# An attention kernel's output store parted over two DMA queues

## The reference

```python
def _L0_xattn_ref(enc_outputs, dec_outputs):
    a_t = jnp.einsum('bed,btd->bet', enc_outputs, dec_outputs)
    a_t = jax.nn.softmax(a_t, axis=-1)
    return jnp.einsum('bet,bed->btd', a_t, enc_outputs)

def _L0_ffn_ref(x, W, b, V_r, C):
    base = jnp.einsum('bsd,od->bso', x, W) + b
    correction = jnp.einsum('bsr,or->bso', jnp.einsum('bsd,dr->bsr', x, V_r), C)
    return base + correction

x = x + _L0_xattn_ref(ctx_1024, _layernorm(x, axis=-1))       # x 1x128x256, ctx 1x12544x256
x = x + _L0_attn_ref(_layernorm(x, axis=-1), w_attn, b_attn, w_proj, b_proj)   # causal, 16 heads
x = x + _L0_ffn_ref(_layernorm(x, axis=-1), W, b, V_r, C)
return x
```

## Time and profile before

| | us |
|---|---|
| time before, median of 3 executions | 106.11 |
| lowest and highest of them | 105.77, 106.12 |
| the profiled execution, its own time | 105.76 |
| its span, first to last instruction | 103.7 |
| around the span (105.76 - 103.7) | 2.06 |
| TensorE busy | 98.3 (95%) |
| the end of `x3`'s instruction in the profile (101.06 + 0.48) | 101.54 |
| the store, from issue to landing | 1.7 |

### The profile page before, as it was taken

One profiled execution on the slowest core, in us unless ns is written; L12 is line 12 of the kernel. 1 busy time (PEld: TensorE's weight loads), 2 busy tenths in 40 slices (PEclk: granted clock), 3 DMA queues, 4 the chain that ended last, 5 costly groups with the idle time before them and its releaser, 6 DMA issues.

```text
span 103.7 us, 2257 instructions
## 1 busy us (share of the span) xinstructions
PE 98.3 (95%) x740; PEld 86.4 (83%) x740; DVE 76.3 (74%) x217; ACT 72.7 (70%) x268; POOL 63.8 (62%) x46
## 2 busy tenths in 40 slices
PE   5999999999999999999999999999999999969990
PEld 1389999999999999999999999999998976845660
DVE  0412959959999999988777797777889745699641
ACT  4019599599999999997777977778879304489410
POOL 6405499869999999999766797666886001004020
PEclk9999999999999999999999999999999999999999
DMA  3899999999999999999999999993000000000001
GB/s 70 330 417 412 411 411 406 408 408 408 414 400 409 403 416 406 408 409 409 408 406 406 411 408 409 388 369 125 0 0 6 0 0 0 0 0 0 6 0 51
DMA packets 8746, 27.86 MB, mean 269 GB/s; under 512 B 1120, under 2 KB 1824, under 8 KB 8736
## 3 DMA queue, kind: packets, MB, share of 16 engines
q1 hardware_dynamic: 8736, 27.73, 68.3%
HBM read 27.59 MB, written 0.13 MB: 267 GB/s over the span
## 4 chain that ended last, share of the span: by engine, by line
PE 89%; DVE 4%; DMA 2%; issue 1%; POOL 1%; ACT 0%; DVEq 0%
PE bank L323 43%; PE bank L335 21%; PE bank L338 10%; DVE head_max L716 2%; DMA x<-x_dram 2%; PE bank L406 2%; PE bank L443 1%; PE bank L344 1%; PE bank L419 1%; PE bank L500 1%; PE bank L308 1%; PE bank L486 1%; PE bank L389 1%; PE bank L386 1%; PE bank L462 1%
## 5 line engine op out<-in xcount | busy, mean ns | idle before, releaser
L288 POOL TENSOR_TENSOR rows_split<-rows_ring,rows_split 128x1024 fp32r<-128x1024 f32 (+1 forms) x25 | 58.4, 2335 | 16.9 <-ACT rows_split L518 16.8
L323 PE MATMUL bank<-query_t,cols_ring 128*128 128x128 f32 x392 | 47.5, 276 | 0.0
L323 PEld LDWEIGHTS bank<-query_t,cols_ring 128*128 128x128 f32 x392 | 45.7, 192 | 1.3 <-ACT query_t L509 0.3
L529 ACT ACTIVATE bank<-bank,neg_max 128x128 f32<-128x128 f32 x98 | 33.1, 338 | 7.4 <-DVE neg_max L653 7.2
L335 PE MATMUL bank<-rows_split,probs 128*128 128x512 f32 x92 | 34.7, 413 | 0.0
L518 ACT CAST rows_split<-rows_ring 128x1024 fp32r<-128x1024 f32 (+1 forms) x25 | 25.8, 1033 | 6.1 <-DMA rows_ring<-ctx_rows_dram 5.1
L670 DVE SCALAR_TENSOR_TENSOR probs<-bank,inv_sums,probs 128x128 fp32r<-128x128 f32 x98 | 27.6, 345 | 0.9
L338 PE MATMUL bank<-rows_split,probs 128*128 128x256 f32 x92 | 25.6, 279 | 0.0
L653 DVE TENSOR_REDUCE neg_max<-bank 128x4 f32<-128x512 f32 (+1 forms) x25 | 16.8, 672 | 8.6 <-PE bank L323 8.6
L335 PEld LDWEIGHTS bank<-rows_split,probs 128*128 128x128 f32 x92 | 17.3, 189 | 3.1
L529 ACT ACTIVATION_READ_ACCUMULATOR bank<-bank,neg_max 128x1 f32 x98 | 19.8, 202 | 0.0
(11 more groups left out here) (96 smaller groups left out, 64.0 us busy)
## 6 DMA issues: line engine op xcount, KB each, us to landing
cols_ring<-ctx_cols_dram SPq DMA_DIRECT2D x24, 512.0 KB, 14.8
rows_ring<-ctx_rows_dram SPq DMA_DIRECT2D x24, 512.0 KB, 15.2
wqk_sb<-w_qk_dram SPq DMA_DIRECT2D x1, 512.0 KB, 11.6
cols_ring<-ctx_cols_dram SPq DMA_DIRECT2D x1, 256.0 KB, 11.3
rows_ring<-ctx_rows_dram SPq DMA_DIRECT2D x1, 256.0 KB, 12.1
wv_sb<-w_v_dram SPq DMA_DIRECT2D x1, 256.0 KB, 11.7
wproj_sb<-w_proj_dram SPq DMA_DIRECT2D x1, 256.0 KB, 10.4
wffn_sb<-w_ffn_dram SPq DMA_DIRECT2D x1, 256.0 KB, 9.7
```

Source lines behind the costliest of these rows:

```text
L288: pool.tensor_tensor(rows_split[:, b, 0:n, 1, :], rows_ring[:, slot * STEP:slot * STEP + n, :], rows_split[:, b, 0:n, 0, :].bitcast(F32), ...
L323: last = pe.matmul(into[:, t * P:(t + 1) * P], cols_ring[:, slot * STEP + t, c, :], query_t[:, c, :], start=(c == 0), stop=(c == DC - 1))
L529: last = act.activation(on[:, t * P:(t + 1) * P], on[:, t * P:(t + 1) * P], ACT.Exp, bias=neg_max[:, b, t:t + 1], accum_out=sums[:, b, t:t ...
```

## The change

The store is parted by rows. SyncE stores rows 0 to 63 (64 KB), ScalarE rows 64 to 127 (64 KB), each after its own wait for `x3_ready`. Both raise the same semaphore by 16, and SyncE now waits for 32. ScalarE's two instructions stand behind all else in its block. `x3` itself is still written by one instruction of all 128 partitions.

```diff
             sp.wait_ge(x3_ready, 1)
-            sp.dma_start(out, x3[:]).then_inc(out_stored, 16)
-            sp.wait_ge(out_stored, 16)
+            sp.dma_start(out[0:P // 2], x3[0:P // 2]).then_inc(out_stored, 16)
+            sp.wait_ge(out_stored, 32)
...
             for c in range(DC):
                 act.wait_ge(x2_t_ready, c + 1)
                 act.copy(x2_centred_t[:, c, :], x2_t_ps[c][:, 0:P]).then_inc(x2_t_copied, 1)
+
+            act.wait_ge(x3_ready, 1)
+            act.dma_start(out[P // 2:P], x3[P // 2:P]).then_inc(out_stored, 16)
```

## The result

The changed kernel takes 106.49 us (median of 22, 105.92 to 107.52), the kernel before 106.03 (median of 22, 105.46 to 106.46). The ratio is 1.0047 with a 95% interval of 1.003 to 1.0063: it is slower by about 0.5 us, and that is clear of the noise. (The longest reading, 107.52, counts as a slow run, and the ratio leaves it out.) I had forecast no change, +0.1. The time lies in the range, and the difference just inside my half per cent, but the forecast of a change too small to see was wrong.

What follows compares the result with a forecast made beforehand. TensorE, busy 95% of the span, was taken to bound the kernel, with the uncovered store at the end the only part touched. Terms 0 + 0 + 0 + 0.1 + 0 + 0 gave +0.1, forecast 106.1 us, range 105.6 to 106.8.

Steps and rivals of the forecast that it cites:

- What bounds the end: From x3's end to the closing barrier: nothing covers the steps, so any change there goes to the time one for one.
- SyncE's store of 64 rows: SyncE's issue of the half store: same 0.37 us as the whole store's; ends -0.18 and 0, taken as 0.
- The bytes: Moving the store's 131 KB: DMA engines already busy throughout, so the same 0.48 us by either queue; taken as 0.
- When ScalarE's half starts: Start of ScalarE's issue relative to SyncE's: 0 if side by side, +0.17 if in line; taken as +0.1 us.
- ScalarE's wait and issue: ScalarE's new instructions at the end: they delay nobody and its later drain stays hidden before the barrier; no cost.
- the completion: SyncE's wait for 32 counts from two transfers: ends 0 and +0.35 us, taken as 0.
- a queue used for the first time: ScalarE's queue carrying its only transfer: being first costs about 0.1 us, within the +0.1 already taken.
- outside the span: The 2.06 us around the profiled span: a second queue could add 0 to +2.06; taken as 0.
- A: Both issues at once, costing by the row, halves earlier by 0.18: -0.1 to -0.2 us, 105.8 to 106.0; chance 0.27.
- B: ScalarE's issue is dear, handled more slowly than SyncE's: an issue of 1.29 would give +0.68 us, 106.7; chance 0.10.
- C: The second queue lengthens the 2.06 us outside the span: +0.53 to +1, 106.6 to 107.0; chance 0.04.
- D: Waits before and behind the bytes go by a transfer's rows, so half would go: -0.6 us, 105.4; chance 0.04.

## Why the prediction was wrong

*What bounds the end* was right. Nothing covers the string from x3 to the barrier, and the +0.49 in it came out one for one in the time.

*SyncE's store of 64 rows* was the step that failed, and ScalarE's with it, which is of 64 rows too. I bounded it by -0.18 and 0 and took 0, arguing that an issue does not follow the bytes. It does not, yet its shape matters: 0.52 in place of 0.37, and the first bytes, which I tied to the end of the issue, came 0.3 later. My bound from above was no bound. I had excluded a loss because a smaller transfer could surely not cost more, without a row that had its number of partitions. The 0.85 and 1.29 of the 32-row loads I rightly left aside: 32 rows alone took 0.33.

*The bytes* failed as well, and by its own premise. A full share does not mean a full rate. I read the 0.94 to 1.01 in the earlier trace rows as "no gaps, so the same 0.48". The share stayed near 1 (0.77 to 1.10 in the full windows) while the rate fell from 340 to 244 GB/s, about +0.2.

*When ScalarE's half starts* carried my only cost, +0.1, for issues in line. The issues run side by side (0.36 and 0.39 in the store by columns). What goes nearly in line is the bytes: ScalarE's began at least 0.24 behind SyncE's. I had reckoned 0.41 and an idle gap of 0.17. The gap did not come, the second half cost no more than its own bytes, and so this term is about 0. The lock that the Trainium skill's page Trace Analysis, section "DMA Instruction — HWDGE (DVE, Sync)", describes is not to be seen in the length of any issue; whether it is what holds ScalarE's bytes back, no run shows.

*ScalarE's wait and issue*, *the completion*, *a queue used for the first time* and *outside the span* came out as said: 0 or at most the 0.1 of the tail with ScalarE as the only issuer. The drain was hidden though twice as long as I took it, SyncE came 0.4 behind the last byte with 32 counts as with 16, and 2.08 lie around the span.

*The rivals* of the prediction. A, side by side, had the two issues at once right, and their cost by the row and the sign wrong. B gave its slower result to ScalarE; SyncE's issue was as long. C and D did not occur. The Trainium skill's rule on two disjoint partition halves, "Don't bother" (page DMA: Bandwidth & Descriptors, section "Rules for kernel authors"), is borne out and by more than it says: one half alone costs more than the whole.

In sum: I put 0 for the shape of the transfer and +0.1 for the issues in line; the runs showed about +0.3 and +0.2 for the shape and about 0 for the issues. That 106.49 still lies in the range is luck. The likeliest case had ended at 106.4, and what opened the range to 106.8 were rivals B and C, which did not occur.

## What to carry to other kernels

A transfer cut in half is another transfer: before parting a store or load, look for a row with the very number of partitions that the parts will have, and if there is none, let the upper bound stay open. Judge bytes by the rate for a share of 1, not by the share. Where a store ends the program, look for a part that can leave while the rest is still being computed: parting it gained only there, and parts that keep all 128 partitions were the ones without the slow issue here, though parted by columns they moved their bytes at a rate of 291 in place of 340.

## What the runs showed of the hardware

- A store of 64 rows is issued in 0.52 to 0.59 us (seven issues in five profiles) and has its first bytes after 1.18 to 1.26 (the three of the table). With 32, 48, 96 or 128 rows it is 0.33 to 0.40 and 0.83 to 0.90, in queues that have nothing else to do.
- For a share of 1 the 16 DMA engines moved 340 GB/s of rows 0 to 127 in one transfer and 338 of rows 32 to 95, but 238 of rows 0 to 63 alone, 241 of rows 64 to 127 alone and 244 of the two halves together. Of the tile parted by columns they moved 291.
- SyncE and ScalarE issue at the same time without lengthening each other's issue (0.36 and 0.39). ScalarE's bytes come behind SyncE's all the same: 1.13 us or more after the issue of 32 rows, where 32 rows alone took 0.83. Why is open.
- With the whole store from ScalarE's queue the tail was 0.1 longer, in one profile; the timed runs (ratio 0.9993 to 1.0024) don't show it, and it stays open.
